# Third layer's attention: two pairs of score banks in turn, one bank each for the turned probabilities and the preparations

## The chip, the cores and the metric

One core of a Trainium2 chip runs the whole program. The metric is device microseconds of one execution, smaller is better. A core has TensorE (matmuls, which write only into PSUM), VectorE, ScalarE and GpSimd (called POOL in the profile), and SyncE (SP), each with its own queue of instructions; they wait for each other by semaphores. PSUM has eight banks of 512 fp32 values in each of 128 partitions, called 0 to 7 here.

## The reference

The model has four layers of attention and a mixture of experts on 32 batches of 128 tokens with 128 features; everything is fp32. The changed stage is the third layer's attention (`L2_xattn` in the reference, `latent_stage` in the kernel). Per batch, with `x` the 77 context tokens and `latents` the 128 tokens:

```
xn = layernorm(x, ln_x_g, ln_x_b)
ln = layernorm(latents, ln_l_g, ln_l_b)
q = ln @ Wq.T
kv = concatenate([xn @ Wkv.T, ln @ Wlkv.T], axis=1)      # 77 + 128 keys and values
q, k, v = split into 2 heads of 64
qn = rmsnorm(q, qn_g) * SCALE;  kn = rmsnorm(k, kn_g)
attn = einsum('bhid,bhjd->bhij', qn, kn)                 # masked for the 77
attn = softmax(attn, axis=-1)
out = einsum('bhij,bhjd->bhid', attn, v)
return out @ Wo.T + bo                                   # added to the tokens
```

In the same stage the kernel finishes the second layer's experts (gathers their rows, weighs, normalizes and adds them), and after the attention it normalizes the new tokens and computes the third router's logits.

## The kernel before, in words

The 32 batches are taken in eight turns of four. Each engine has its own program, a loop over iterations n from -12 to 38, written out by hand; t = n // 4 is the turn and i = n % 4 the place in it. Iterations below 0 are the head, in which only preparations run. The order of the calls in each loop is the order in that engine's queue; no planner changes it.

The steps of one batch n:

- `scores` (TensorE, iteration n-1): four matmul instructions of the heads' queries and keys into two banks, one head in each (line 1720), and four of the mask (line 1722). Each matmul of the program shows as two in the profile. It waits for `shift` of the batch before, since the two banks are the same for all batches.
- `maximum` and `shift` (VectorE, iteration n): the row maximum out of the score banks (line 1568), and the scores minus it into `soft` in SBUF (line 1572). After this the banks are free.
- `exponents` (ScalarE, n), `invert_sums` (VectorE, n+1, line 1579), `weigh` (ScalarE, n+1, line 1632).
- `turn_probs` (TensorE, n+2): four transposes of the weighted probabilities into one bank (lines 1731 and 1732), two banks in turn. `take_turned` (ScalarE, n+2) copies them out (lines 1638 and 1639).
- `values` (TensorE, n+3, lines 1741 and 1742), `take_attention` (ScalarE, n+3, line 1643), `project` (TensorE, n+3, line 1749), `add` (VectorE, n+3, line 1584), which adds the projection to the tokens.
- `keep_warm` (TensorE, line 1753): one matmul without use in each iteration.

Nine preparations of each turn, called jobs, run on TensorE between these steps, four batches at once. They share two banks in turn: job k uses bank k % 2 and waits until job k-2 has been copied out. In the queue's order they are x (transposes of the normalized tokens, line 1698; ScalarE copies them into `xT`, line 1598), r0 (query, key and value of the first batch, line 1709; ScalarE copies it into `raw`, line 1606), l (logits, line 1694; VectorE, line 1542), r1, r2, r3, k (transposes of the scaled keys, line 1704; VectorE copies them into `keys`, line 1545), q (queries of the four batches, line 1700; ScalarE, line 1601) and t (transposes of the finished tokens, line 1690; ScalarE, line 1596). The jobs x, r and q of a turn run two turns ahead of its attention, k one turn ahead; t and l follow one turn behind. So in turn t of the loop, x, r and q are those of turn t+2, and turns 6 and 7 have none. t and l begin in turn 2.

TensorE's loop, one iteration:

```
values(pe, n - 3)
for job in jobs_at(n, 0): do_job(pe, job)    # i = 2: x      i = 3: r2
turn_probs(pe, n - 2)
for job in jobs_at(n, 1): do_job(pe, job)    # i = 1: t      i = 2: r0, l      i = 3: r3, k
project(pe, n - 3)
scores(pe, n + 1)
keep_warm(pe)
for job in jobs_at(n, 2): do_job(pe, job)    # i = 2: r1     i = 3: q
```

VectorE's loop in one iteration: `maximum` and `shift` of n, at i = 3 `scale_keys` (line 1531, which k needs), `invert_sums` of n-1, at i = 0 the sums of squares (line 1520), at i = 1 `normalize` (line 1513, which x needs), `add` of n-3, the copies of its jobs, and then the rest of the second layer: `combine` (line 1459), `gain` (line 1476) and, at i = 3, `join` (line 1492). ScalarE's loop: `take_attention`, the copies of place 0, `take_turned`, the copies of place 1 (after r3 also the squares of the four batches, line 1610), `exponents`, `weigh`, the copies of place 2. POOL gathers rows by indirect DMAs and takes the reciprocal roots.

The eight banks before: 0 and 1 scores, 2 and 3 turned probabilities, 4 values, 5 projection, 6 and 7 preparations.

Of the kernel before, what the change touches and what calls it, by code (L numbers as in the profile page):

```python
# [15 lines left out]
ALU = mybir.AluOpType  # L16
ACT = mybir.ActivationFunctionType
AX_X = mybir.AxisListType.X

P = 128  # L20
NBATCH = 32
NTURN = NBATCH // 4
NKEY = 77
# [1344 lines left out]
def latent_stage(nc, net, latent, before, behind):  # L1368
# [6 lines left out]
    heads, NK, R = 2, NKEY + P, 4  # L1375

    with ExitStack() as ctx:  # L1377
        def sb(n, shape, dt=F32):
            return ctx.enter_context(nc.sbuf_tensor(f"L2x_{n}", shape, dt))

        def sem(n):
            return net.sem(f"L2x_{n}")

        x, ident = net.x, net.ident
        keys, wqkv = latent.keys, latent.wqkv
        score_ps = net.psum[:, 0:2, :]
        turn_bank, out_bank, proj_bank, prep_bank = net.banks[2:4], net.banks[4], net.banks[5], net.banks[6:8]

        got = [[sb(f"got{i}{k}", [P, 4, P]) for k in range(2)] for i in range(2)]
        y = sb("y", [P, 4, P]); ystats = sb("ystats", [P, 4, 6]); ymean_var = sb("ymean_var", [P, 4, 2]); yrstd = sb("yrstd", [P, 4])  # L1390
# [5 lines left out]
        qT = [sb(f"qT{i}", [P, 4 * P]) for i in range(2)]  # L1396
        soft = [sb(f"soft{i}", [P, heads, NK]) for i in range(4)]
        mx, rsum, rinv = ([sb(f"{n}{i}", [P, heads]) for i in range(2)] for n in ("mx", "rsum", "rinv"))
# [3 lines left out]
        E, wg = behind["E"], latent.wg  # L1402
# [8 lines left out]
        job_ps, keys_out, act_out = sem("job_ps"), sem("keys_out"), sem("act_out")  # L1411
        squared, summed, length_ready, chain3, scaled = (
            sem(n) for n in ("squared", "summed", "length_ready", "chain3", "scaled"))
        scores_ready, max_ready, shifted = sem("scores_ready"), sem("max_ready"), sem("shifted")
        exp_done, inv_ready, probs_ready = sem("exp_done"), sem("inv_ready"), sem("probs_ready")
        turned, turned_out, values_done = sem("turned"), sem("turned_out"), sem("values_done")
# [11 lines left out]
        def jobs_at(n, place):  # L1428
            t, i = n // 4, n % 4
            found = [(t + lag, j) for j, (lag, *at) in places.items() if at == [i, place] and 0 <= t + lag < NTURN]  # L1430
            if place == 1:
                found += [(d, what) for d in range(NTURN) for what, late in (("t", 3), ("l", 4)) if n == place_of(d) + late]
            return found

        HEAD, TAIL = -12, 7
        order = [job for n in range(HEAD, NBATCH + TAIL) for place in range(3) for job in jobs_at(n, place)]
        number = {job: k for k, job in enumerate(order)}

        def by_dve(job):
            return job[1] in ("k", "l")  # L1440

        def outs_by(job):

            some = [by_dve(j) for j in order[:number[job] + 1]]
            return sum(some), len(some) - sum(some)
# [89 lines left out]
        def take_job(dve, job):  # L1535
            if not by_dve(job):
                return
            t, what = job
            k = number[job]
            dve.wait_ge(job_ps, k + 1)  # L1540
            if what == "l":
                dve.tensor_copy(behind["logits"][:, :, 4 * t:4 * t + 4],
                                prep_bank[k % 2][:, 0:4 * E].rearrange("p (b e) -> p e b", b=4)).then_inc(keys_out, 1)
            else:
                dve.tensor_scalar(keys[:, 4 * t:4 * t + 4, NKEY:NK], prep_bank[k % 2][:, :].rearrange("p (b k) -> p b k", b=4),
                                  latent.gq[:, 0:1], latent.gk[:, 0:1], ALU.mult, ALU.mult).then_inc(keys_out, 1)

        def done_variances(dve, t):
# [16 lines left out]

        def maximum(dve, n):
            dve.wait_ge(scores_ready, n + 1)
            dve.tensor_reduce(mx[n % 2][:, :], score_ps[:, :, 0:NK], AX_X, ALU.max).then_inc(max_ready, 1)

        def shift(dve, n):  # L1570
            dve.wait_ge(max_ready, n + 1)
            dve.tensor_tensor(soft[n % 4][:, :, :], score_ps[:, :, 0:NK], mx[n % 2][:, :].unsqueeze(2).to_broadcast([P, heads, NK]),
                              ALU.subtract).then_inc(shifted, 1)

        def invert_sums(dve, n):
# [12 lines left out]
        def take_others(act, job):  # L1588
            if by_dve(job):
                return  # L1590
            t, what = job
            k = number[job]
            bank = prep_bank[k % 2]
            act.wait_ge(job_ps, k + 1)
            if what == "t":
                act.copy(lT[:, :], bank[:, :]).then_inc(act_out, 1)
            elif what == "x":
                act.activation(xT[:, :], bank[:, :], ACT.Identity, scale=latent.lat_g[:, 0:1],
                               bias=latent.lat_b[:, 0:1]).then_inc(act_out, 1)
            elif what == "q":  # L1600
                act.copy(qT[t % 2][:, :], bank[:, :]).then_inc(act_out, 1)
            else:
                b = int(what[1])
                if t >= R and b == 0:
                    act.wait_ge(values_done, 4 * (t - R + 1))
                act.copy(raw[t % R][:, b, :], bank[:, 0:3 * P]).then_inc(act_out, 1)
                if b == 3:
                    act.wait_ge(act_out, outs_by(job)[1])
                    act.wait_ge(summed, t)
                    act.activation(sq[:, :, :], raw[t % R][:, :, 0:2 * P], ACT.Square).then_inc(squared, 1)  # L1610
# [23 lines left out]

        def take_turned(act, n):
            act.wait_ge(turned, n + 1)
            ps = turn_bank[n % 2][:, :].rearrange("p (m t) -> p m t", m=4)
            act.copy(probs_lat[n % 2][:, :, :], ps[:, 0:2, :])
            act.copy(probs_ctx[n % 2][:, :, :], ps[0:NKEY, 2:4, :]).then_inc(turned_out, 1)

# [39 lines left out]
        def do_job(pe, job):  # L1680
            t, what = job
            k = number[job]
            if k >= 2:
                dve_outs, act_outs = outs_by(order[k - 2])
                pe.wait_ge(keys_out, dve_outs) if by_dve(order[k - 2]) else pe.wait_ge(act_out, act_outs)
            bank = prep_bank[k % 2]
            if what == "t":
                pe.wait_ge(normed2, t + 1)
                for b in range(4):
                    last = pe.transpose(bank[:, b * P:(b + 1) * P], behind["routed"].xn[:, 4 * t + b, :], ident[:, :])  # L1690
            elif what == "l":
                pe.wait_ge(act_out, outs_by((t, "t"))[1])
                for b in range(4):
                    last = pe.matmul(bank[:, b * E:(b + 1) * E], lT[:, b * P:(b + 1) * P], wg[:, :], start=True, stop=True)
            elif what == "x":
                pe.wait_ge(normed, t + 1)
                for b in range(4):
                    last = pe.transpose(bank[:, b * P:(b + 1) * P], xn[t % 2][:, b, :], ident[:, :])
            elif what == "q":
                last = pe.matmul(bank[:, :], wqkv[:, 0:P], xT[:, :], start=True, stop=True)  # L1700
            elif what == "k":
                pe.wait_ge(scaled, t + 1)
                for b in range(4):
                    last = pe.transpose(bank[:, b * P:(b + 1) * P], kn[:, b, :], ident[:, :])
            else:
                b = int(what[1])
                if b == 0:
                    pe.wait_ge(act_out, outs_by((t, "x"))[1])
                last = pe.matmul(bank[:, 0:3 * P], xT[:, b * P:(b + 1) * P], wqkv[:, :], start=True, stop=True)
            last.then_inc(job_ps, 1)  # L1710

        def scores(pe, n):
            t, b = n // 4, n % 4
            pe.wait_ge(shifted, n)
            if b == 0:
                pe.wait_ge(keys_out, outs_by((t, "k"))[0])
                pe.wait_ge(act_out, outs_by((t, "q"))[1])
            for i in range(heads):
                rows = slice(64 * i, 64 * i + 64)
                pe.matmul(score_ps[:, i, 0:NK], qT[t % 2][rows, b * P:(b + 1) * P], keys[rows, n, :], start=True, stop=False)  # L1720
            for i in range(heads):
                last = pe.matmul(score_ps[:, i, 0:NKEY], net.ones_row[:, :], latent.mask_row[:, n, :], start=False, stop=True)
            last.then_inc(scores_ready, 1)

        def turn_probs(pe, n):
            pe.wait_ge(probs_ready, n + 1)
            if n >= 2:
                pe.wait_ge(turned_out, n - 1)
            bank = turn_bank[n % 2]
            for i in range(heads):  # L1730
                pe.transpose(bank[:, i * P:(i + 1) * P], soft[n % 4][:, i, NKEY:NK], ident[:, :])
                last = pe.transpose(bank[0:NKEY, (2 + i) * P:(3 + i) * P], soft[n % 4][:, i, 0:NKEY], ident[:, :])
            last.then_inc(turned, 1)
# [1878 lines left out]
```

## Time and profile before

| | |
|---|---|
| time, median of 3 runs | 2423.79 us (2410.94, 2423.79, 2427.91) |
| profiled execution: span from first to last instruction | 2408.2 us |
| profiled execution: its own time | not marked among the three; the fastest lies 2.7 us above the span |
| TensorE matmuls, busy | 1980.2 us (82%) |
| VectorE, busy | 1543.5 us (64%) |
| ScalarE, busy | 1111.0 us (46%) |
| GpSimd, busy | 989.2 us (41%) |
| mean granted clock of TensorE | 0.916 of 2.4 GHz |

Busy shares are means over many stages with different limits; they don't say what binds the changed stage. Times in the profile's rows are microseconds from the start of the span, and a matmul's duration contains its way through the array, so that the durations of consecutive matmuls overlap.

### The profile page before, as it was taken

The page shows a single profiled execution, that of the slowest core. Times are in us where ns is not written, and L with a number is a line of the kernel's source. Part 1 is how long each engine was busy: PE and PEld are TensorE (multiplying, and loading weights), DVE is VectorE, ACT ScalarE, POOL GpSimd, SP SyncE. Part 2 cuts the span into 40 slices and gives each one's busy share as a digit, 9 for nine tenths or more (in the row PEclk, how much of TensorE's full clock was granted, in tenths as well). Part 3 has the DMA queues.
Part 4 walks back from the last instruction along what each step waited for, and adds up shares of the span by engine and source line. Part 5 has one row for each costly group of instructions (what it writes and reads, how often), then busy time and mean ns, then how long its engine had stood idle before and what let it go on. Part 6 is the DMA issues. An engine that isn't in the chain of part 4 may idle for free. (4 is left out here: it accounts for less than half of the span.)

```text
span 2408.2 us, 39264 instructions
## 1 busy us (share of the span) xinstructions
PE 1980.2 (82%) x14419; PEld 1400.9 (58%) x14419; DVE 1543.5 (64%) x3706; ACT 1111.0 (46%) x2201; POOL 989.2 (41%) x886
## 2 busy tenths in 40 slices
PE   5887799799999976854593898799589888879998
PEld 3666599667777754431592555567367566654443
DVE  6996522368787755969314885511598699866775
ACT  4886444244444432225331665423244567644443
POOL 3554165344443214647566741271675200112332
PEclk9997799899999988975796999899699999999999
DMA  3000478321112125979891100342231100012221
GB/s 113 1 2 2 146 242 245 103 70 59 59 56 75 37 67 178 327 255 309 264 325 53 26 12 1 128 126 78 68 122 49 41 2 2 2 36 75 80 80 48
DMA packets 138277, 238.45 MB, mean 99 GB/s; under 512 B 20755, under 2 KB 66748, under 8 KB 133970
## 3 DMA queue, kind: packets, MB, share of 16 engines
q1 hardware_dynamic: 114216, 173.65, 21.7%
q0 software_dynamic: 23872, 62.29, 9.2%
q8 instruction: 116, 1.90, 0.3%
q14 instruction: 73, 0.60, 0.1%
HBM read 161.89 MB, written 73.99 MB: 98 GB/s over the span
## 5 line engine op out<-in xcount | busy, mean ns | idle before, releaser
L432 POOL TENSOR_TENSOR L1x_soft<-L1x_soft,L1x_rinv 128x616 f32<-128x616 f32 x64 | 77.6, 1214 | 190.8 <-DVE L1x_rinv L355 190.7
L2153 ACT ACTIVATE L3f_hT<-banks,L3f_b 128x512 f32<-128x512 f32 x128 | 87.9, 687 | 136.9 <-PE banks L2172 130.1
L2098 DVE TENSOR_TENSOR L3f_hT<-L3f_hT,L3f_spread 128x512 f32<-128x512 f32 x128 | 99.8, 802 | 35.1 <-ACT L3f_hT L2153 32.7
L2185 PE MATMUL banks<-L3f_hT,L3f_w 128*128 128x512 f32 x256 | 121.4, 598 | 0.0
L2172 PE MATMUL banks<-L3f_xT,L3f_w 128*128 128x512 f32 x256 | 120.1, 593 | 0.6 <-PEq L730 0.6
L2663 POOL DMA_INDIRECT L0e_rows<-xn_rows,L0f_token_of x78 | 77.9, 999 | 98.0 <-issue 61.7
L887 POOL TENSOR_TENSOR L0x_soft<-L0x_soft,L0x_rinv 128x1232 f32<-128x1232 f32 x32 | 71.9, 2247 | 99.7 <-DVE L0x_rinv L812 99.7
L2982 ACT ACTIVATE L0e_hT<-banks,L0e_w 128x256 f32<-128x256 f32 x156 | 69.1, 473 | 88.3 <-PE banks L3025 88.3
L404 ACT COPY L1x_attnT<-banks 128x512 f32<-128x512 f32 x64 | 37.5, 585 | 148.2 <-PE banks L513 148.2
L2663 POOL DMA_INDIRECT L1h_rows<-xn_rows,L1f_token_of x72 | 73.9, 1026 | 77.8 <-POOLq L2416 46.7
L266 DVE COPY L1x_keys<-banks 128x308 f32<-128x308 f32 x112 | 52.0, 464 | 69.0 <-PE banks L461 68.9
L2663 POOL DMA_INDIRECT L2e_rows<-xn_rows,L2f_token_of x64 | 63.9, 999 | 69.6 <-POOLq L2416 39.4
L425 POOL DMA_INDIRECT L3x_got<-rows,L2f_slot_read x64 | 65.1, 1018 | 64.7 <-POOLq L61 49.0
L3339 POOL DMA_INDIRECT L1o_hid<-mixed,L1f_token_of x72 | 71.8, 997 | 44.0 <-issue 21.8
L2998 DVE TENSOR_TENSOR L0e_y<-banks,L0e_w 128x256 f32<-128x256 f32 x39 | 16.5, 424 | 114.3 <-PE banks L3034 114.3
L861 ACT COPY L3s_probsT<-banks 128x512 f32<-128x512 f32 x128 | 68.7, 591 | 44.3 <-PE banks L936 44.3
L485 PE MATMUL banks<-L1x_keys,L1x_xT 128*128 128x308 f32 x256 | 82.1, 443 | 7.4 <-DVE L1x_soft L346 6.7
L425 POOL DMA_INDIRECT L1x_got<-rows,L0f_slot_read x64 | 65.3, 1021 | 51.6 <-POOLq L61 36.2
L3208 POOL DMA_INDIRECT L1m_got<-hidden,L1f_slot_read x64 | 68.4, 1069 | 41.9 <-POOLq L3060 22.7
L461 PE MATMUL banks<-context,L1x_a 96*128 96x308 f32 x224 | 81.9, 448 | 4.2 <-DVE L1x_keys L266 4.2
L2172 PEld LDWEIGHTS banks<-L3f_xT,L3f_w 128*128 128x128 f32 x256 | 48.6, 190 | 61.5 <-issue 61.5
L1652 POOL DMA_INDIRECT L2x_got<-rows,L1f_slot_read x64 | 66.0, 1032 | 36.6 <-SPq L1377 19.4
(600 smaller groups left out, 5850.9 us busy)
## 6 DMA issues: line engine op xcount, KB each, us to landing
hidden<-L1h_hid SPq DMA_DIRECT2D x24, 768.0 KB, 5.0
L0e_w<-in_L0f_w SPq DMA_DIRECT2D x39, 320.0 KB, 4.7
L0e_w<-in_L0f_w SPq DMA_DIRECT2D x39, 258.0 KB, 3.8
L1x_flat_values<-L1x_staged SPq DMA_DIRECT2D x34, 256.0 KB, 2.0
L1x_vals<-L1x_flat_values SPq DMA_DIRECT2D x14, 616.0 KB
mixed<-L1m_out SPq DMA_DIRECT2D x32, 256.0 KB, 4.0
L3f_spread<-L3f_gates SPq DMA_DIRECT2D x8, 1024.0 KB, 7.4
L3x_keys<-L_keys SPq DMA_DIRECT2D x5, 1232.0 KB
```

The costliest lines, as they stand in the source:

```text
L425: pool.indirect_dma_start(got[g % 8][k][:, :], None, pre["rows"][:, :], bass.IndirectOffsetOnAxis(pre["routed"].read[:, g, k:k + 1], 0), b ...
L432: pool.tensor_tensor(tile, tile, rinv[n % 2][:, :].unsqueeze(2).to_broadcast([P, U, NK]), ALU.mult).then_inc(probs_ready, 1)
L461: last = pe.matmul(bank[:, 0:4 * NK], a[:, i, :], context[:, 4 * t:4 * t + 4, :], start=True, stop=True)
L485: last = pe.matmul(score_ps[:, i, 0:4 * NK], xT[t % 2][:, b * P:(b + 1) * P], keys[t % 2][:, U * u + 4 * i:U * u + 4 * i + 4, b, :], start ...
L887: pool.tensor_tensor(tile, tile, rinv[g % 2][:, :].unsqueeze(2).to_broadcast([P, heads, NK]), ALU.mult).then_inc(probs_ready, 1)
L2098: dve.tensor_tensor(tile, tile, spread[t % 2][:, e, :], ALU.mult).then_inc(weighed, 1)
L2153: act.activation(hT[m % 3][:, c, :], hid_bank[(FC * m + c) % 4][:, :], ACT.Relu, bias=b1[:, FC * e + c:FC * e + c + 1]).then_inc(hid_out, 1)
L2172: pe.matmul(hid_bank[n % 4][:, :], w1[:, e, c * P:(c + 1) * P], xT[t % 2][:, :], start=True, stop=True).then_inc(hid_ready, 1)
L2185: last = pe.matmul(bank[:, :], w2[:, e, c, :], hT[m % 3][:, c, :], start=False, stop=(e == E - 1 and c == FC - 1))
L2663: return pool.indirect_dma_start(out, None, net.xn_rows[:, :], bass.IndirectOffsetOnAxis(routed.token_of[:, tile:tile + 1], 0), bounds_che ...
L2982: act.activation(hT[j % 2][:, c, :], hid_bank[c][:, 0:Q * P], ACT.Gelu, bias=w1[j % R][:, FC * P + c:FC * P + c + 1]).then_inc(hid_out, 1)
L3339: pool.indirect_dma_start(hid[e % N][:, q, :], None, mixed_dram[:, :], bass.IndirectOffsetOnAxis(routed.token_of[:, Q * e + q:Q * e + q + ...
```

## The change

The two banks of the scores become two pairs, used by even and odd batches in turn (0 and 1, 2 and 3). `scores` of batch n now waits for `shift` of batch n-2 in place of n-1. In exchange the turned probabilities have one bank (4) in place of two, so that `turn_probs` of batch n waits until batch n-1 has been copied out, and the preparations have one bank (7) in place of two, so that each job waits until the job before it has been copied out. Values and projection move to banks 5 and 6. No computation is added, removed or moved in any queue.

```
-        score_ps = net.psum[:, 0:2, :]
-        turn_bank, out_bank, proj_bank, prep_bank = net.banks[2:4], net.banks[4], net.banks[5], net.banks[6:8]
+        score_ps = [net.psum[:, 0:2, 0:NK], net.psum[:, 2:4, 0:NK]]
+        turn_bank, out_bank, proj_bank, prep_bank = net.banks[4], net.banks[5], net.banks[6], net.banks[7]
...
-            dve.tensor_reduce(mx[n % 2][:, :], score_ps[:, :, 0:NK], AX_X, ALU.max).then_inc(max_ready, 1)
+            dve.tensor_reduce(mx[n % 2][:, :], score_ps[n % 2], AX_X, ALU.max).then_inc(max_ready, 1)
...
-            ps = turn_bank[n % 2][:, :].rearrange("p (m t) -> p m t", m=4)
+            ps = turn_bank[:, :].rearrange("p (m t) -> p m t", m=4)
...
-            if k >= 2:
-                dve_outs, act_outs = outs_by(order[k - 2])
-                pe.wait_ge(keys_out, dve_outs) if by_dve(order[k - 2]) else pe.wait_ge(act_out, act_outs)
-            bank = prep_bank[k % 2]
+            if k:
+                dve_outs, act_outs = outs_by(order[k - 1])
+                pe.wait_ge(keys_out, dve_outs) if by_dve(order[k - 1]) else pe.wait_ge(act_out, act_outs)
+            bank = prep_bank
...
-            pe.wait_ge(shifted, n)
+            if n >= 2:
+                pe.wait_ge(shifted, n - 1)
...
-                pe.matmul(score_ps[:, i, 0:NK], qT[t % 2][rows, b * P:(b + 1) * P], keys[rows, n, :], start=True, stop=False)
+                pe.matmul(score_ps[n % 2][:, i, :], qT[t % 2][rows, b * P:(b + 1) * P], keys[rows, n, :], start=True, stop=False)
...
-            if n >= 2:
-                pe.wait_ge(turned_out, n - 1)
-            bank = turn_bank[n % 2]
+            if n:
+                pe.wait_ge(turned_out, n)
+            bank = turn_bank
```

The lines left out change `shift`, `take_job`, `take_others` and the mask's matmuls to the same banks.

## Rows read from the trace of the kernel before

**Rows 1.** The page's chain of the work that ended last, by line.

```profile
PE banks L2185 5%; PE banks L2172 5%; PE banks L2182 0%; PE banks L2056 0%; PE banks L2192 0%; PE banks L2062 0%; PE banks L2048 0%; POOLq L3519 0%; POOL L3f_out_n L2136 0%; POOL L3f_out_n L2139 0%; POOL L3f_rstd L2131 0%; DVE L3f_stats L2110 0%; DVE L3f_out_n L2123 0%; DVE L3f_acc L2103 0%; ACT L3f_yT L2160 0%
```

**Rows 2.** Timeline: start, us, engine, line, operation, [idle before, releaser]; the stage's ends.

```profile
1290.44 0.61 DVE L1459 SCALAR_TENSOR_TENSOR L2x_y<-L2x_got,L1f_gate,L1f_xn_all 128x128 f32<-128x128 f32 x2 [16.67 <-DMA L2x_got<-rows,L1f_slot_read]
...
1508.84 2.02 PE L2357 MATMUL banks<-L3x_wqT,L3x_wkT 64*96 64x128 f32 x16 [0.60 <-PEq L1377]
```

**Rows 3.** List of waits, turn 0 (1325 to 1348.3): total, times, longest.

```profile
PE banks L1720 <- DVE L2x_soft L1572: 3.7, 2, 3.2
```

**Rows 4.** List of waits, turns 1 to 3 (1348.3 to 1413.5).

```profile
DVE x L1584 <- PE banks L1749: 7.0, 6, 1.5
...
PE banks L1720 <- DVE L2x_soft L1572: 2.4, 3, 1.2
```

**Rows 5.** List of waits, turns 4 to 7 (1413.5 to 1490).

```profile
PE banks L1720 <- DVE L2x_soft L1572: 0.4, 1, 0.4
```

**Rows 6.** Timeline of turn 3, iteration 2: r0, l, their copy, the addition.

```profile
1404.52 0.88 PE L1709 MATMUL banks<-L_wqkv,L2x_xT 128*128 128x384 f32 x2 [0.52 <-ACT L2x_xT L1598]
...
1405.24 0.95 PE L1694 MATMUL banks<-L_wg,L2x_lT 128*128 128x8 f32 x8
...
1405.44 0.48 ACT L1606 COPY L2x_raw<-banks 128x384 f32<-128x384 f32 x1 [0.54 <-PE banks L1709]
...
1406.55 0.29 DVE L1584 TENSOR_TENSOR x<-x,banks 128x128 f32<-128x128 f32 x1 [1.51 <-PE banks L1749]
```

**Rows 7.** Timeline of turn 3, iteration 3: r2's copy, r3, k, keys, join, scores.

```profile
1410.62 0.48 ACT L1606 COPY L2x_raw<-banks 128x384 f32<-128x384 f32 x1 [0.56 <-PE banks L1709]
...
1410.86 0.81 PE L1709 MATMUL banks<-L_wqkv,L2x_xT 128*128 128x384 f32 x2
...
1411.43 0.43 PEld L1704 LDWEIGHTS banks<-ident,L2x_kn 128*128 128x128 f32 x4 [0.38 <-ACT L2x_raw L1606]
...
1412.57 0.81 DVE L1545 TENSOR_SCALAR L_keys<-banks,L_gq,L_gk 128x512 f32<-128x512 f32 x1
...
1413.29 1.13 DVE L1492 SCALAR_TENSOR_TENSOR x<-L2x_y,L2x_yrstd,x 128x128 f32<-128x128 f32 x4
...
1413.48 0.62 PE L1720 MATMUL banks<-L_keys,L2x_qT 64*128 64x205 f32 x4 [1.15 <-issue]
```

**Rows 8.** Timeline of the head: the r jobs of turns 0 and 1, k, join.

```profile
1305.96 4.72 PE L1709 MATMUL banks<-L_wqkv,L2x_xT 128*128 128x384 f32 x8 [0.87 <-ACT L2x_xT L1598]
...
1307.65 0.48 ACT L1606 COPY L2x_raw<-banks 128x384 f32<-128x384 f32 x1 [1.74 <-PE banks L1709]
...
1312.32 1.22 DVE L1520 TENSOR_REDUCE L2x_length<-L2x_sq 128x16 f32<-128x1024 f32 x1 [1.18 <-ACT L2x_sq L1610]
...
1318.70 5.16 PE L1709 MATMUL banks<-L_wqkv,L2x_xT 128*128 128x384 f32 x8 [0.96 <-ACT L2x_xT L1598]
...
1323.45 0.60 PEld L1704 LDWEIGHTS banks<-ident,L2x_kn 128*128 128x128 f32 x4 [0.44 <-ACT L2x_raw L1606]
...
1324.34 0.81 DVE L1545 TENSOR_SCALAR L_keys<-banks,L_gq,L_gk 128x512 f32<-128x512 f32 x1 [3.55 <-PE banks L1704]
...
1325.07 2.94 DVE L1492 SCALAR_TENSOR_TENSOR x<-L2x_y,L2x_yrstd,x 128x128 f32<-128x128 f32 x4
```

**Rows 9.** Timeline of turn 0: `normalize` for x2, and x2's transposes.

```profile
1334.82 1.10 DVE L1513 TENSOR_SCALAR L2x_xn<-x,L2x_mean_var,L2x_rstd 128x128 f32<-128x128 f32 x4
...
1338.37 1.06 PE L1698 MATMUL banks<-ident,L2x_xn 128*128 128x128 f32 x4
```

**Rows 10.** Windows: stretch, length, busy us (instructions) by engine, granted clock, DMA.

```profile
1330.00:1341.00 11.00, 9.70 (x30) 5.96 (x30) 10.09 (x37) 4.14 (x13) 9.78 (x8) 0.53 0.10 25
1341.00:1415.00 74.00, 65.42 (x411) 42.74 (x410) 60.91 (x236) 50.98 (x151) 49.79 (x42) 1.00 0.10 24
1415.00:1419.00 4.00, 4.00 (x17) 2.06 (x16) 3.38 (x14) 0.85 (x2) 1.42 (x2) 0.57 0.00 0
...
1459.00:1463.40 4.40, 4.40 (x17) 2.23 (x17) 2.60 (x6) 1.27 (x4) 1.39 (x1) 0.61 0.00 0
```

More of the change, by code:

```diff
@@ L1542, in take_job @@
                 dve.tensor_copy(behind["logits"][:, :, 4 * t:4 * t + 4],
-                                prep_bank[k % 2][:, 0:4 * E].rearrange("p (b e) -> p e b", b=4)).then_inc(keys_out, 1)
+                                prep_bank[:, 0:4 * E].rearrange("p (b e) -> p e b", b=4)).then_inc(keys_out, 1)
             else:
-                dve.tensor_scalar(keys[:, 4 * t:4 * t + 4, NKEY:NK], prep_bank[k % 2][:, :].rearrange("p (b k) -> p b k", b=4),
+                dve.tensor_scalar(keys[:, 4 * t:4 * t + 4, NKEY:NK], prep_bank[:, :].rearrange("p (b k) -> p b k", b=4),
                                   latent.gq[:, 0:1], latent.gk[:, 0:1], ALU.mult, ALU.mult).then_inc(keys_out, 1)
@@ L1567, in maximum @@
             dve.wait_ge(scores_ready, n + 1)
-            dve.tensor_reduce(mx[n % 2][:, :], score_ps[:, :, 0:NK], AX_X, ALU.max).then_inc(max_ready, 1)
+            dve.tensor_reduce(mx[n % 2][:, :], score_ps[n % 2], AX_X, ALU.max).then_inc(max_ready, 1)
         def shift(dve, n):
             dve.wait_ge(max_ready, n + 1)
-            dve.tensor_tensor(soft[n % 4][:, :, :], score_ps[:, :, 0:NK], mx[n % 2][:, :].unsqueeze(2).to_broadcast([P, heads, NK]),
+            dve.tensor_tensor(soft[n % 4][:, :, :], score_ps[n % 2], mx[n % 2][:, :].unsqueeze(2).to_broadcast([P, heads, NK]),
                               ALU.subtract).then_inc(shifted, 1)
@@ L1682, in do_job @@
             k = number[job]
-            if k >= 2:
-                dve_outs, act_outs = outs_by(order[k - 2])
-                pe.wait_ge(keys_out, dve_outs) if by_dve(order[k - 2]) else pe.wait_ge(act_out, act_outs)
-            bank = prep_bank[k % 2]
+            if k:
+                dve_outs, act_outs = outs_by(order[k - 1])
+                pe.wait_ge(keys_out, dve_outs) if by_dve(order[k - 1]) else pe.wait_ge(act_out, act_outs)
+            bank = prep_bank
             if what == "t":
@@ L1719, in scores @@
                 rows = slice(64 * i, 64 * i + 64)
-                pe.matmul(score_ps[:, i, 0:NK], qT[t % 2][rows, b * P:(b + 1) * P], keys[rows, n, :], start=True, stop=False)
+                pe.matmul(score_ps[n % 2][:, i, :], qT[t % 2][rows, b * P:(b + 1) * P], keys[rows, n, :], start=True, stop=False)
             for i in range(heads):
-                last = pe.matmul(score_ps[:, i, 0:NKEY], net.ones_row[:, :], latent.mask_row[:, n, :], start=False, stop=True)
+                last = pe.matmul(score_ps[n % 2][:, i, 0:NKEY], net.ones_row[:, :], latent.mask_row[:, n, :], start=False, stop=True)
             last.then_inc(scores_ready, 1)
```

## The prediction

> **What bounds the kernel now.** I read the page first. Its chain of the work that ended last has 5% each on lines 2172 and 2185, the last layer's experts, and no line of the changed stage [rows 1]; of this stage it says nothing. What matters is that the stage is closed: VectorE begins it after a wait of 16.67 us for the gathered rows, and the next stage's first matmuls at 1508.84 come after a barrier [rows 2]. Every microsecond that the stage loses or gains should reach the end unchanged.
>
> Inside the stage I read the list of waits, cut by turns (four batches each), and then the timeline. TensorE waits for VectorE's shift ahead of the score matmuls: 3.7 us in turn 0, 2.4 us in turns 1 to 3, 0.4 us afterwards, 6.5 us in all in six places [rows 3 to 5]. That is all that a second pair of score banks can remove. The same list has two waits that stay. Ahead of the first scores of a turn TensorE stands 1.15 us, because they need the keys that VectorE has just copied; the row [rows 7] stands for seven, turns 1 to 7. And VectorE stands ahead of its addition at line 1584 until TensorE's projection is done, 7.0 us in turns 1 to 3 [rows 4]: at iterations 2 and 3 of a turn TensorE is the late one, and any delay of a projection is handed to VectorE.
>
> **The score banks: what is removed.** In turns 1 to 5 the removed waits are 2.4 + 0.4 = 2.8 us. The work queued behind them (the next transposes, the copy into xT, r0) follows on TensorE and ends in the addition for which VectorE waited 1.51 us [rows 6], so I count the 2.8 us in full. The wait of scores n+1 for shift n becomes one for shift n-1. That is already implied: the transposes of batch n-2 earlier in TensorE's order need the weighted probabilities, which need the reciprocal behind shift n-1. So no wait replaces it. In turn 0 the 3.7 us are worth less, as the matter of the first turn shows below. DMAs and the queues of SP and POOL are not touched.
>
> **The turned bank: nothing.** Transposing batch n-2 now waits until batch n-3 has been copied out. The value matmuls of batch n-3, which stand ahead of it in the same iteration, wait for the same copy. Without that cover it would cost one pair of ScalarE copies.
>
> **The preparation bank: what is added.** A turn has nine jobs, in the order x, r0, l, r1, r2, r3, k, q, t. Each now waits for the copy of the one before it. Six of the waits I count at nothing: r0 already needs the copy of x as data; q comes behind the first scores, which need the copy of k; r1, t and x have scores, keep-warm matmuls and values between them and the job before, which cover a copy; and r2 loaded its weights in the same hundredths in which r1's copy ended. Three stand too close.
>
> l: r0's copy runs from 1405.44 to 1405.92, and l's first matmul started at 1405.24 [rows 6]. It can start some 0.1 us after the copy, so 0.8 us late; the projection behind it, and VectorE's addition, follow. l meets an r0 in turns 2 to 5: 4 x 0.8 = 3.2 us.
>
> r3 and k: r2's copy ends at 1410.62 + 0.48 = 1411.10, and r3's matmuls started at 1410.86 [rows 7], so r3 moves by 0.35 us to 1411.2. They take 0.81, the copy 0.48: it ends at about 1412.55, and k's weights, which loaded at 1411.43, load at 1412.6. k is late by 1.2 us. Behind k stand the projection, then VectorE's addition, then the copy of the keys (0.81 us, from 1412.57), then the first scores at 1413.48 [rows 7]. All are in one chain, so turn after turn starts 1.2 us later: five times in turns 1 to 5, 6.0 us, and once in turn 0. Turns 6 and 7 have no r jobs and lose nothing.
>
> The turns 1 to 5 together: 6.0 + 3.2 - 2.8 = +6.4 us.
>
> The head runs two sets of jobs with nothing between them. A cold pass from r00's first matmul to the end of its copy is 1305.96 to 1308.13, 2.17 us [rows 8]; a warm one, r0 in turn 3, 1404.52 to 1405.92, 1.40 us [rows 6]. First set: four passes end at 1305.96 + 4 x 2.17 = 1314.6, with two warm ones at 1313.1; before, the run ended at 1310.68 and its last copy about 0.5 later. That is +3.5 or +1.9; I take +3.0. It goes on through the squares, for which VectorE waited 1.18 us [rows 8]. Second set: from r10 to k's weights it was 1318.70 to 1323.45, 4.75 us; four cold passes take 8.7, two cold and two warm 7.1: +3.9 or +2.4. Its eight matmuls took 5.16 us, 0.645 each, all cold, so I take +3.5. VectorE waited 3.55 us for k there [rows 8], so this passes on too. Then its joining step took 2.94 us, against 1.13 us in a turn [rows 7, 8]; moved by 6 us it may lose that disturbance, -1.8 to 0; I take -1.5, as 1.13 is its size in the turns. VectorE enters turn 0 late by 3.0 + 3.5 - 1.5 = 5.0 us (2.5 to 7.4).
>
> The first turn has the slack of the removed score waits. The transposes of x2 started at 1338.37; their input was ready at 1334.82 + 1.10 = 1335.92 [rows 9]. With the score waits gone only that input holds them: 1335.92 + 5.0 = 1340.9, +2.5 us (0 to 4.9). With k's 1.2 us turn 0 costs +3.7.
>
> **Clock.** The granted clock was 0.53 between 1330 and 1341 and fell to 0.57 and 0.61 for about 4 us in two places, the first just behind a 1.15 us wait at the first scores of a turn; between 1341 and 1415, with three such waits in it, it was 1.00 [rows 7, 10]. One fall costs some 4.00 x (1 - 0.57) = 1.7 us. The waits of l, r3 and k add gaps around those places; I take one fall more, +1.7 us, bounds -3.4 (none left) to +8.5 (five more). The Trainium skill (TensorE: Matmul & The Clock Gate, Part 1) says that activity releases the throttle and idleness brings it back. By that alone every turn would have to fall; the rows show two.
>
> Sum: 3.7 + 6.4 + 1.7 = 11.8 us. The profiled execution's span is 2408.2 us, 2.7 below the fastest of the three runs and 15.6 below their median; which run it was is not marked. As the sum is a difference, I set it on the median: 2423.8 + 11.8 = 2436 us.
>
> A rule speaks against the half that gives up banks. The Trainium skill (Perfetto Trace Analysis, Optimizing Tensor Performance) wants independent matmul groups to rotate through banks, so that copying one out overlaps the next group's matmuls. By it each of the nine jobs pays its copy; it is the third rival.
>
> **Rivals.** Low clock: the added gaps keep TensorE at 1.2 GHz through half of each of turns 0 to 5. For: the falls follow waits. Against: seven turns start after 1.15 us, two fall. Price: about 10 us a turn at 0.57, 4.3 each, 26 in all above the 10.1 without falls: 2460.
>
> Full clock, which ends not slower: the early scores fill turn 0 and the gaps, and TensorE is granted 2.4 GHz from the head on. The head's passes then take 1.40: the first set ends 0.4 late, the second gains 0.85, the join gives back 1.8, so x2 is no longer late but up to 3.0 early, the half-speed work up to 1341 shrinks by 1.2, and both falls vanish (-3.4). With +1.2 and +6.4 this is 0.0: 2424. It decides if VectorE's first maximum comes no later than in the old trace. Against: the second set of the head ran dense and still cold.
>
> Every copy exposed: nine copies at 0.48, 4.3 us a turn instead of 2.0, because ScalarE comes late to each. In turns 0 to 5 that is 14 us more: 2450. Against: ScalarE stood idle ahead of the copy of r0 [rows 6].
>
> The change does not do what it says: the early scores only move the wait to the next transposes. Then the 2.8 us stay lost: 2439, inside the range.
>
> **How the numbers follow.** Forecast 0.68, low clock 0.10, full clock 0.12, every copy exposed 0.04, wait only moved 0.06. The forecast's own bounds are 0 + 1.2 + 6.4 - 3.4 = +4 and 4.9 + 1.2 + 6.4 + 8.5 = +21, 2428 to 2445; the runs of one kernel spread over 17 us, so half of that goes to either side: 2420 to 2453, which also takes in the full clock's 2424 and the exposed copies' 2450 and leaves out the low clock. One per cent, 24 us, is about what a measurement here can tell. Slower by more than that: 2448 and above, low clock 0.10, exposed copies 0.03, the forecast's upper edge 0.05: 0.18. Faster by over 1% needs a gain of which the six waits hold a quarter: 0.02. The rest, 0.80, is within.
>
> **What would show it.** No wait of line 1720 for line 1572 in turns 1 to 7. Waits of l's, r3's and k's weight loads for ScalarE's line 1606, 0.8, 0.4 and 0.8 us. The copies of the head's r jobs 2.2 us apart instead of 1.28 or less. VectorE's first maximum about 5 us later against the stage's start, the first scores of turn 6 about 10 to 12 us later, and the stage's last two turns as long as before. I am wrong if the clock in the stage is granted otherwise than here, or if VectorE, not TensorE, turns out to set iterations 2 and 3, so that a delayed k costs less than it is late.

## The result and the profile after

The changed kernel takes 2441.14 us (median of 4 runs, 2436.81 to 2445.82) against 2425.24 us for the kernel before in the same session (2410.94 to 2427.91): a ratio of 1.0082, 95% interval 1.0062 to 1.0103. By this interval it is slower by 15 to 25 us, by the medians 15.9: inside the forecast range, and more than the forecast 11.8.

The profiled execution of the changed kernel took 2445.82 us with a span of 2444.0, the longest of its four; that of before, by its span of 2408.2, was the shortest of its own. So I read the stage by itself, from VectorE's first combine to the next stage's first matmuls (before: [rows 2]). Behind line 1713 the numbers are one higher than before. Timeline of the changed kernel (columns as in [rows 2]), the two ends of the stage:

```profile
1296.41 0.61 DVE L1459 SCALAR_TENSOR_TENSOR L2x_y<-L2x_got,L1f_gate,L1f_xn_all 128x128 f32<-128x128 f32 x2 [16.77 <-DMA L2x_got<-rows,L1f_slot_read]
...
1540.49 2.02 PE L2358 MATMUL banks<-L3x_wqT,L3x_wkT 64*96 64x128 f32 x16 [0.59 <-PEq L1377]
```

That is 244.1 us where it was 218.4 [rows 2], 25.7 more. The list of waits of the changed kernel from 1340 to 1526 (releaser, total, times, longest) has none of the scores (now line 1721) for line 1572 any more; the 1.15 us ahead of the first scores of each turn have stayed, and three new ones have come:

```profile
DVE x L1584 <- PE banks L1750: 46.6, 23, 5.3
...
PE banks L1721 <- issue: 8.0, 7, 1.1
...
PEld banks L1704 <- ACT L2x_raw L1606: 7.1, 6, 1.2
...
PEld banks L1694 <- ACT L2x_raw L1606: 4.7, 4, 1.2
...
PEld banks L1709 <- ACT L2x_raw L1606: 2.4, 8, 0.4
```

k waits in six turns, l in the four in which it meets an r0, and r2 and r3 0.3 us each, all for ScalarE's copy: the places that the forecast named, and r2 besides. The first line shows where it ends: VectorE stands longer ahead of its addition. The same line of the kernel before, from 1326 to 1494, the same part of its stage:

```profile
DVE x L1584 <- PE banks L1749: 29.9, 20, 3.7
```

Head of the changed kernel, timeline (before: [rows 8]):

```profile
1314.21 1.65 PE L1709 MATMUL banks<-L_wqkv,L2x_xT 128*128 128x384 f32 x2 [0.57 <-ACT L2x_raw L1606]
...
1315.90 0.48 ACT L1606 COPY L2x_raw<-banks 128x384 f32<-128x384 f32 x1 [1.74 <-PE banks L1709]
...
1318.12 0.48 ACT L1606 COPY L2x_raw<-banks 128x384 f32<-128x384 f32 x1 [1.74 <-PE banks L1709]
...
1321.93 1.22 DVE L1520 TENSOR_REDUCE L2x_length<-L2x_sq 128x16 f32<-128x1024 f32 x1 [5.07 <-ACT L2x_sq L1610]
...
1338.32 0.81 DVE L1545 TENSOR_SCALAR L_keys<-banks,L_gq,L_gk 128x512 f32<-128x512 f32 x1 [7.94 <-PE banks L1704]
1339.05 1.13 DVE L1492 SCALAR_TENSOR_TENSOR x<-L2x_y,L2x_yrstd,x 128x128 f32<-128x128 f32 x4
```

The copies come 2.22 us apart. The sums of squares start 25.5 us behind the stage's start instead of 21.9, the keys 41.9 instead of 33.9, and VectorE's first maximum, at 1341.61, 45.2 instead of 39.0.

The clock tells the rest. Windows of the kernel before over its head (columns as in [rows 10]), a stretch that the prediction did not use:

```profile
1308.44:1316.44 8.00, 3.29 (x7) 1.13 (x6) 6.58 (x28) 3.18 (x6) 6.39 (x7) 0.92 0.12 34
1316.44:1322.44 6.00, 4.82 (x10) 2.78 (x11) 4.17 (x19) 1.73 (x3) 5.07 (x5) 0.51 0.16 44
1322.44:1329.44 7.00, 4.12 (x17) 2.00 (x16) 4.99 (x15) 3.88 (x5) 4.32 (x4) 0.93 0.15 37
1330.44:1340.44 10.00, 9.14 (x29) 5.70 (x29) 9.68 (x36) 3.62 (x12) 8.78 (x8) 0.50 0.11 28
```

The same part of the changed kernel, up to the point where its clock rises:

```profile
1314.41:1322.41 8.00, 6.29 (x8) 1.81 (x8) 2.82 (x15) 2.49 (x4) 6.57 (x7) 0.50 0.12 33
1322.41:1335.41 13.00, 6.99 (x12) 2.69 (x12) 7.68 (x31) 2.92 (x6) 8.36 (x9) 0.50 0.14 36
1335.41:1361.70 26.29, 24.71 (x70) 13.25 (x70) 16.90 (x56) 10.54 (x27) 15.73 (x13) 0.50 0.10 22
```

Before, the clock rose to 2.4 GHz within the last microsecond of each dense run of eight r matmuls [rows 8], and 50 us behind the stage's start the clock rose for the turns. With 0.57 us of waiting ahead of every pair of them it stays at 1.2 GHz for the whole head and most of turn 0, until 65 us behind the start (58 us in the repeat below). Windows of the changed kernel by turns (first scores to first scores; the last one ends with the stage):

```profile
1339.21:1365.61 26.40, 24.57 (x76) 13.75 (x76) 17.14 (x58) 12.51 (x34) 14.58 (x12) 0.57 0.09 20
1365.61:1386.81 21.20, 18.85 (x114) 11.69 (x115) 17.92 (x72) 14.20 (x44) 15.79 (x13) 1.00 0.11 26
1386.81:1411.71 24.90, 21.95 (x126) 13.60 (x127) 19.08 (x77) 14.90 (x45) 15.74 (x13) 0.93 0.09 22
1411.71:1438.21 26.50, 23.59 (x126) 14.19 (x126) 19.29 (x77) 14.69 (x45) 13.53 (x11) 0.87 0.08 16
1438.21:1463.11 24.90, 21.93 (x126) 13.65 (x127) 19.30 (x77) 14.76 (x45) 7.20 (x5) 0.93 0.00 1
1463.11:1489.61 26.50, 23.58 (x126) 14.10 (x126) 14.39 (x54) 14.71 (x45) 6.67 (x4) 0.87 0.00 1
1489.61:1509.31 19.70, 18.03 (x114) 11.75 (x114) 11.09 (x36) 11.80 (x40) 5.80 (x3) 0.91 0.01 1
1509.31:1540.51 31.20, 24.11 (x174) 17.39 (x174) 13.24 (x56) 14.30 (x48) 2.08 (x3) 0.93 0.00 1
```

Length times (1 - clock) is what a turn would have been shorter at full clock if TensorE's work alone set its length; I call it the low clock's share, and an upper bound. In turns 1 to 6 it is 12.0 us here (turn 3: 26.50 x 0.13 = 3.4) and was 3.4 in the same view of before. Read in windows of 1 us, these are seven falls of 3.4 us each at 1.2 GHz where before had two of the same length [rows 10]: four begin 1.1 to 2.1 us behind the first scores of turns 3 to 6, three some 16 to 18 us into turns 2, 3 and 5, within 2 us behind l.

### The profile page after: what moved, and what is told of

Same layout as the page of the kernel before. It is cut to its first block and busy times, and to the rows that moved or that the text cites. A ratio compares the mean times of both kernels' runs of the same rounds, so it can differ in the third digit from the quotient of the medians.

```text
span 2444.0 us, 39266 instructions
## 1 busy us (share of the span) xinstructions
PE 2011.3 (82%) x14419; PEld 1411.7 (58%) x14419; DVE 1544.4 (63%) x3706; ACT 1111.3 (45%) x2201; POOL 987.0 (40%) x886
## 5 line engine op out<-in xcount | busy, mean ns | idle before, releaser
L425 POOL DMA_INDIRECT L3x_got<-rows,L2f_slot_read x64 | 65.2, 1019 | 64.7 <-POOLq L61 49.0
L425 POOL DMA_INDIRECT L1x_got<-rows,L0f_slot_read x64 | 65.3, 1021 | 54.9 <-POOLq L61 39.5
L3209 POOL DMA_INDIRECT L1m_got<-hidden,L1f_slot_read x64 | 67.8, 1060 | 41.2 <-POOLq L3061 21.9
L3026 PE MATMUL banks<-L0e_xT,L0e_w 128*128 128x256 f32 x312 | 78.0, 395 | 4.2 <-DMA L0e_w<-in_L0f_w 4.1
```

The costliest lines, as they stand in the source:

```text
L425: pool.indirect_dma_start(got[g % 8][k][:, :], None, pre["rows"][:, :], bass.IndirectOffsetOnAxis(pre["routed"].read[:, g, k:k + 1], 0), b ...
L3026: pe.matmul(hid_bank[c][:, 0:Q * P], w1[j % R][:, c * P:(c + 1) * P], xT[j % 2][:, :], start=True, stop=True).then_inc(hid_ready, 1)
```

## The experiments

All stages are measured from the first combine; "falls" are returns to 1.2 GHz in turns 1 to 6 (in turn 7 every kernel has some, 5 to 16 us long in all up to the end of the stage). Theory A says that the handovers of the single preparation bank cost some 10 us by themselves and that the gaps they open cost at least as much again through the clock. The main rival says that the handovers alone are the cost and the falls cost nothing; a second, that the halved turned bank or the score pairs do it.

**Pairs alone.** Score pairs and one turned bank as in the change, but two preparation banks; to find the room, projections go to the output's bank, and the keep-warm matmuls write to the turned bank:

```
turn_bank, out_bank, proj_bank, prep_bank = net.banks[4], net.banks[5], net.banks[5][:, P:2 * P], net.banks[6:8]
```

> The two pairs of score banks are kept, the preparations have their two banks again; values and projection share a bank, and the keep-warm matmuls write into the bank of the turned probabilities. Theory A (the loss comes from the preparations' single bank, and from the lower clock that its gaps bring; the pairs and the single turned bank are harmless): the stage, 218.4 us from the first combine to the next stage's matmuls before and 244.1 us after, comes to 213 to 218 us, the run is 0 to 6 us faster than before, and TensorE doesn't wait for the shift (line 1572) ahead of the scores. Rival B (running the scores ahead itself disturbs the stage: VectorE or the clock): the stage stays above 228 us and the run is 10 us or more slower than before.

2416.8 against 2420.26 us, ratio 0.9984 [0.9968, 0.9999]; stage 217.7 us, first maximum 38.9, two falls. One wait for the shift, of 1.23 us, is left, in turn 0. Half of the change costs nothing and gains a little; the turned bank is cleared of suspicion.

**One preparation bank alone.** The kernel before, with this half of the change:

```
-            if k >= 2:
-                dve_outs, act_outs = outs_by(order[k - 2])
...
-            bank = prep_bank[k % 2]
+            if k:
+                dve_outs, act_outs = outs_by(order[k - 1])
...
+            bank = prep_bank
```

> Only the preparations lose a bank; scores and turned probabilities are as before. Theory A: the whole loss of the change and the small gain missing, a stage of 240 to 250 us, 15 to 25 us slower than before. Rival B: a stage under 228 us, less than 8 us slower.

2445.64 us, ratio 1.0111 [1.0085, 1.0137]; stage 248.8, first maximum 45.1, seven falls, four of them of 6.8 us. The whole loss is here.

The next three keep both banks and add the wait for the job before to some jobs only, so that its parts can be told apart.

**Head alone:** jobs of the two sets ahead of the turns wait as in the change.

```
for late in ((1, 2) if (t == 0 and what != "t" and what != "l") or (t == 1 and what in ("x", "r0", "r1", "r2", "r3", "q")) else (2,)):
```

> The kernel before with both preparation banks, but in the head (the jobs x, r0 to r3, q of turns 0 and 1, and k of turn 0) each job also waits for the copy of the job before. Theory A (handovers add up, and a head that is not dense leaves TensorE at 1.2 GHz longer): first maximum 6 us later against the stage's start, the first scores of turn 1 10 to 12 us later, the stage 226 to 231 us. Rival C (the handovers alone count, the clock recovers as before): first maximum 6 us later, but the slack of turn 0 takes some of it, so turn 1 is 4 to 6 us later and the stage is 222 to 225 us.

2424.88 us, ratio 1.0023 [1.0007, 1.0040]; stage 229.5, first maximum 45.2, first scores of turn 1 at 65.2 us instead of 57.8. The clock is 0.50 through the head here too, until 59 us behind the start: the head's waits hold it down, and nothing in the turns does. Theory A's first maximum and stage came; turn 1 came 7.3 us later, between its 10 to 12 and rival C's 4 to 6.

**r2, r3 and k alone:**

```
for late in ((1, 2) if (t >= 2 and what in ("r2", "r3")) or (t >= 1 and what == "k") else (2,)):
```

> The kernel before with both preparation banks, but from the loop on the jobs r2, r3 (of turns 2 to 7) and k (of turns 1 to 7) also wait for the copy of the job before. Theory A as forecast (1.2 us in each of turns 0 to 5): 7 us, a stage of 225 to 226 us, with two or three falls of the clock. Rival D (the gaps bring falls of the clock, 1.7 us each, in most turns): 12 to 17 us, a stage of 230 to 236 us, and five or more falls.

2434.56 us, ratio 1.0070 [1.0043, 1.0096]; stage 238.0, six falls, one of them of 6.8 us: a low clock's share of 12.0 us for the 3.4 of before, the same in its repeat below. Rival D's falls came, and its 236 us were passed. Without the low clock's share (half of the time at 1.2 GHz, here and below) turns 0 to 5 take 131.5 us against 125.9 and 126.2 in the two executions of before: 5.3 to 5.6 us for the forecast's 1.2 x 6 = 7.2, and 4.1 to 4.5 of it in turns 1 to 5.

**The gaps filled at l, r3 and k.** The changed kernel with a useless matmul ahead of each (of 256 columns; in the head of 128, ahead of r1 and r2 too):

```
+            if what in ("l", "r3", "k") or (n < 0 and what in ("r1", "r2")):
...
+                pe.matmul(out_bank[:, P:(1 + c) * P], ident[:, :], ident[:, :].unsqueeze(1).to_broadcast([P, c, P]), start=True, stop=True)
```

> The changed kernel as it is, but ahead of l, r3 and k (in the head also r1 and r2) TensorE runs one matmul without use (256 columns; 128 in the head) into the values' bank, in the time in which it would wait for the copy. Theory A, with the falls of the clock as the larger part of the loss: the clock falls in two or three of the turns 1 to 7 in place of seven, and the stage is 226 to 236 us in place of 244.1; the 6 us of the three handovers in the turns stay. Rival C (the falls have another cause, the handovers are dearer than they look): six or more falls, a stage of 243 us or more.

2437.21 us, ratio 1.0064 [1.0043, 1.0084]; stage 241.0, five falls. A miss for both: most falls stayed, and the stage lies between the two. Read by place, though, four of the five now begin within 2 us behind the first scores of a turn, whose 1.15 us wait had not been filled, and only one behind l.

**l alone:**

```
for late in ((1, 2) if what == "l" else (2,)):
```

> The kernel before with both preparation banks, but the job l also waits for the copy of the job before it. Theory A: 0.8 us in each of the turns 2 to 5, a stage of 221 to 222 us with the two falls that there were, 3 us over the kernel before; one fall more would make it 224. Rival: it is hidden behind VectorE, 218 to 219 us.

2429.57 us, ratio 1.0024 [1.0010, 1.0039]; stage 230.0, three falls, some 17 us into turns 2, 3 and 4, just behind l, two of them of 6.8 us. The stage is well above the expected 221 to 222, but not for l's own wait: without the low clock's share turns 1 to 5 take 111.6 us against 108.0 and 108.4 before, so 3.1 to 3.5 us for the forecast 3.2. The rest is mostly falls, which l's wait brings besides, and 1.4 to 1.5 us of the head, which runs ahead of the first l and in which the clock was low for 10.2 us in place of 6.8 between the two r runs.

**Pairs alone, first scores filled.** One line into the version with pairs alone:

```
             if b == 0:
+                keep_warm(pe, n - 1)
                 pe.wait_ge(keys_out, outs_by((t, "k"))[0])
```

> The run with the pairs alone, and one keep-warm matmul more (384 columns) ahead of the first scores of each turn, where TensorE waits 1.15 us for the keys. Theory A (the falls come behind this wait): at most one fall in the turns 1 to 7, a stage of 210 to 214 us, 5 to 9 us faster than before. Rival: the wait isn't what the clock falls for, 216 to 219 us, as without.

2412.8 against 2421.1 us, ratio 0.9964 [0.9951, 0.9978]; stage 215.7, above the expected 210 to 214, and no fall. This version beats both kernels. What the filling alone adds to the pairs alone is not clear of noise: the two ratios' intervals overlap, and of the two falls that went only one had begun behind the first scores.

**The kernel before again.**

> The kernel before, profiled once more, to see how far the stage and its falls differ between two executions. Theory A: the stage within 3 us of 218.4, with one to three falls in the turns 1 to 7, and the head and turn 0 the same to 0.5 us. Rival: the stage differs by 8 us or more, so that a single profile of it can't carry the experiments.

2421.6 us; stage 223.3, two falls and a longer one in turn 7. The stage of one kernel differs by 4.9 us between two executions, more than the 3 us expected; most of that is the low clock's share over turns 0 to 7, 12.5 and 16.7 us.

**The changed kernel with its first scores filled,** and **the changed kernel again.** The edit is the line above, as `keep_warm(pe)`.

> The changed kernel with one keep-warm matmul more ahead of the first scores of each turn. Theory A (in turns 1 to 7 the change costs three handovers plus falls of the clock, and a matmul in the wait of the first scores stops the falls): no fall in turns 1 to 7, the stage shrinks from 244 us to 228 to 234 us; what is left above the 215.7 us of the version with pairs alone and the same filling is the head (5 us at the first maximum), the later x2 of turn 0 and the handovers (about 2 us a turn). Rival B (handovers alone, the falls cost nothing): the stage stays at 240 to 246. Rival C (the change's falls start at l, r3 and k and the filling doesn't reach them): four or more falls stay, 238 to 244.

> The changed kernel again, one look, for the spread of its stage from run to run: 236 to 246 us (244.1 in the first profile), first maximum 45 us behind the stage's start, 5 to 8 falls in turns 1 to 7. If the stage is under 236, the first profile was an extreme one and its excess over the forecast is chance.

The first: 2435.57 us against 2418.68, ratio 1.0066 [1.0049, 1.0083]; stage 240.2. Theory A's number missed, rival C's fits: the falls behind the first scores are gone and four are left, one in each of turns 2 to 5, three of them of 6.8 us, so that the low clock's share of turns 1 to 6 is 12.0 us as in the first profile. Timeline of this version, TensorE in turn 2:

```profile
1389.88 0.88 PE L1709 MATMUL banks<-L_wqkv,L2x_xT 128*128 128x384 f32 x2 [0.52 <-ACT L2x_xT L1598]
1391.33 1.15 PE L1694 MATMUL banks<-L_wg,L2x_lT 128*128 128x8 f32 x8 [0.57 <-ACT L2x_raw L1606]
1392.33 0.78 PE L1751 MATMUL banks<-L_wo,L2x_attnT 128*128 128x128 f32 x2
1393.04 1.05 PE L1722 MATMUL banks<-L_keys,L2x_qT 64*128 64x205 f32 x4
```

r0 has waited 0.52 us for the copy of x, as it did before [rows 6], and l 0.57 for the copy of r0; two matmuls of the projection then take 0.78 us instead of the 0.39 of full clock. The second: 2444.78 us, stage 248.8, above the expected 246, so the long stage of the first profile is no accident. Both profiled executions of the changed kernel lie near the upper end of its runs, though (2436.81 to 2445.82), and its median run may have a shorter stage.

**Filled ahead of r0 and l as well,** and **everywhere at once:**

```
+            if n >= 0 and what in ("r0", "l"):
...
+                pe.matmul(out_bank[:, P:(1 + c) * P], ident[:, :], ident[:, :].unsqueeze(1).to_broadcast([P, c, P]), start=True, stop=True)
```

This condition is that of the first; the second's takes in r3 and k too, and r1, r2, r3 and k of the head. Both fill the first scores.

> The version with the filled first scores, and one useless matmul of 256 columns more ahead of r0 and of l in the turns. With the first scores filled, four falls were left, one in each of turns 2 to 5, each within 5 us behind l, in the turns in which l waits 0.57 us right behind r0's wait of 0.52 us. Theory A2 (this pair of waits sets those falls off): no fall or one in turns 2 to 5, each of these turns 23 to 24 us instead of 24.9 to 26.4, the stage 230 to 235 us. Rival C2 (the falls of turns 2 to 5 come from the sum of the added waits, l's, r3's and k's, wherever they lie): three or four falls stay or move to r3 and k, the stage 239 to 243.

> The changed kernel with useless matmuls ahead of every waiting place at once: the first scores, r0, l, r3 and k of the turns and r1, r2, r3 and k of the head. Theory A (clock): no fall in turns 1 to 7; the stage 229 to 236 us, where what is left above the 215.7 us of the version with pairs alone and filled is the handovers themselves and the fillers that lie on the path. Rival C (waits at the handovers and not the clock are the cost): still 238 us or more with no fall left. Rival D (the clock falls without regard to such waits): four or more falls left.

2426.5 us, ratio 1.0035 [1.0016, 1.0054], stage 231.0; and 2425.77 us, ratio 1.0015 [0.9999, 1.0032], stage 229.9. One fall is left in each, in turn 4. Windows of the first of the two, turns 2 to 5:

```profile
1373.87:1397.17 23.30, 21.92 (x134) 13.77 (x134) 19.09 (x77) 14.86 (x45) 15.78 (x13) 1.00 0.10 23
1397.17:1420.47 23.30, 21.92 (x134) 13.77 (x134) 19.28 (x77) 14.87 (x45) 13.66 (x11) 1.00 0.08 18
1420.47:1445.27 24.80, 23.46 (x132) 14.43 (x132) 19.08 (x77) 14.84 (x45) 7.20 (x5) 0.93 0.01 1
1445.27:1468.57 23.30, 21.92 (x132) 13.77 (x132) 14.27 (x54) 14.74 (x45) 6.68 (x4) 1.00 0.00 1
```

With useless work added, turns 2, 3 and 5 are 3.1 us shorter each than with the first scores alone filled (26.4). Theory A is borne out, and the rival that the falls cost nothing is refuted. Filling r3, k and the head too changes the stage by 1 us: with the waits of r0, l and the first scores filled, those of r3 and k bring no falls of their own.

They are not harmless for that. Falls that begin within 2.2 us behind the first scores of turns 1 to 6 number two, one, one, two and none in the five versions whose r2, r3 and k don't wait in the turns (before twice, pairs alone, head alone, l alone), and four, five, four, five and four in the five whose do (the changed kernel twice, one preparation bank alone, r2, r3 and k alone, l, r3 and k filled). The 1.15 us wait is in all ten; more falls follow it where these jobs wait ahead of it, and in all four versions that fill it no such fall is left. At l it is the added wait: with l alone made to wait, three of turns 2 to 5 have a fall behind it. r0 and l were filled only together, so that what filling one of them would do beside filled first scores is not shown.

## Why the prediction was right in direction and too small

The terms of the sum against the stage, twice: the first profiles, and the two repeats. Each is a difference of the stretch's length, with the low clock's share of turns 1 to 7 taken out into rows of its own. The stage was longer by 25.7 and 25.5 us in these pairs of executions, the medians of the runs by 15.9; so the rows show where the loss lies, and more of it than a median run has.

| term | forecast | 244.1 - 218.4 | 248.8 - 223.3 |
|---|---|---|---|
| to the first scores of turn 1 | 3.7 | 11.4 | 8.6 |
| turns 1 to 5 without low clock | 6.4 | 5.8 | 5.0 |
| turns 6 and 7 without low clock | 0 | 1.7 | 0.0 |
| low clock, turns 1 to 6 | 1.7 | 8.5 | 12.0 |
| low clock, turn 7 | 0 | -1.7 | -0.1 |
| sum | 11.8 | 25.7 | 25.5 |

**Right: the handovers.** l, r3 and k wait where forecast, the projection and VectorE's addition follow, and turns 1 to 5 without the low clock come out at 5.0 to 5.8 us for 6.4. In part that is luck, since two of its terms were too large and have opposite signs. l alone measured 3.1 to 3.5 for 3.2. r3 and k measured 4.1 to 4.5 for 6.0. The score pairs were counted at 2.8 us there; the version with pairs alone shows 1.4 to 1.8 (106.6 for 108.0 and 108.4 us), and there the shared output bank and its wait are included. The parts add up: one preparation bank alone takes 115.5 us there, 7.1 to 7.5 more than before. No wait took the place of the shift's, and the turned bank cost nothing. The rival of nine exposed copies is out: only l, r2, r3 and k show an added wait in the turns. The Trainium skill (Perfetto Trace Analysis, Optimizing Tensor Performance) wants groups to rotate through banks; the head agrees, where a pass takes 2.22 us between copies instead of the 1.28 that it took at the same low clock with two banks.

**Right in size: the head.** First set +3.6 for 3.0; keys +8.0, so +4.4 in the second part for 3.5; the join took 1.13 instead of 2.94 us, -1.8 for -1.5; VectorE's first maximum +6.2 for 5.0, within 2.5 to 7.4.

**Wrong: the first turn.** The step "with the score waits gone only that input holds them", +2.5 for x2's transposes, failed. They started at 1350.33, 53.9 us behind the start instead of 47.9: +6.0. Their input accounts for +3.8 of that, since the first maximum came 6.2 us late and not 5.0. But it was not the input that held them, as the changed kernel's timeline shows:

```profile
1346.99 1.10 DVE L1513 TENSOR_SCALAR L2x_xn<-x,L2x_mean_var,L2x_rstd 128x128 f32<-128x128 f32 x4
...
1348.89 1.65 PE L1754 MATMUL banks<-ident 128*128 128x384 f32 x2
...
1350.33 1.06 PE L1698 MATMUL banks<-ident,L2x_xn 128*128 128x128 f32 x4
```

The input was there at 1348.09, and TensorE came 2.24 us after it. The join's gain is VectorE's alone; TensorE began turn 0 when the keys came, 8.0 us late, and its first scores and the queries behind them now ran at half speed. Before, then after:

```profile
1325.25 0.62 PE L1720 MATMUL banks<-L_keys,L2x_qT 64*128 64x205 f32 x4 [0.95 <-issue]
...
1326.39 1.12 PE L1700 MATMUL banks<-L2x_xT,L_wqkv 128*128 128x512 f32 x2
...
1330.69 1.05 PE L1720 MATMUL banks<-L_keys,L2x_qT 64*128 64x205 f32 x4 [3.18 <-DVE L2x_soft L1572]
```

```profile
1339.18 1.05 PE L1721 MATMUL banks<-L_keys,L2x_qT 64*128 64x205 f32 x4 [0.91 <-DVE L_keys L1545]
...
1341.23 2.08 PE L1700 MATMUL banks<-L2x_xT,L_wqkv 128*128 128x512 f32 x2
...
1343.23 1.05 PE L1721 MATMUL banks<-L_keys,L2x_qT 64*128 64x205 f32 x4
```

From its first scores to x2's transposes TensorE needed 13.12 us before, 3.68 of them waits for the shift, and 11.15 after, without a wait: 3.68 us of waits removed were worth 1.97. Where the clock was back in time the step held: in the version with r0 and l filled the queries took 1.13 us, and x2 started 0.14 us behind its input. Behind x2 come the other 5.4 of the 11.4 us, 1.2 of them forecast for k: the half-speed stretch lasted 15 us longer than before (9 in the repeat). I had taken the head as cold in the old kernel and read its clock only from 1330 on; it had two stretches at full clock, the second up to the first scores and queries of turn 0, and the change removed both. That the clock is granted otherwise than in the rows was one of my own signs of being wrong. With all gaps filled the clock was back 38 us behind the start, and turn 1 came 4.8 us late, close to the forecast 3.7. With the same head and only l, r3 and k filled it was back as early, but low again for 10.2 us from 51 us on, and turn 1 came 7.7 us late.

**Wrong: "I take one fall more, +1.7 us".** That term measured 8.5 and 12.0 us. The price of a fall was right, 1.7 us for 3.4 us at half speed. Their number was not: five more in the first profile, exactly the bound of +8.5 that I had put at the edge, and in the repeat seven falls of which two are twice as long. With it the stage's 25.7 and 25.5 us lie above my own upper bound of +21; that the time lies well inside the range is owed to the median run, which lost 15.9, and there is luck in that. The low-clock rival, with its price of 26 us, named the mechanism; a third to a half of it happened, and in other places, at the first scores and behind l. The Trainium skill (TensorE: Matmul & The Clock Gate, Part 1) says that idleness brings the throttle back. The trace agrees on the direction: pairs of waits of 0.52 and 0.57 us were followed by falls, and filling them took three of four away. That one follows every wait, as I had read it, is not so: in the changed kernel turn 1, with its waits at the first scores and at k, stayed at 1.00.

**Open.** Why the fall of turn 4 stays with every place filled; why the falls behind the first scores stayed with l, r3 and k filled; and why the clock rises 42 us behind the start in the version with r0 and l filled but at 57 us with the first scores alone filled, although TensorE's program is the same up to there (the changed kernel itself had 65 and 58). The 6.0 us by which the changed kernel reached the stage later are not the change's: the unchanged work ahead of it ended between 1288.8 and 1298.2 in these executions.

## What to carry to other kernels

A buffer taken from a dense TensorE run was paid twice here, once for the copy that is exposed and once for the clock: read the granted clock over every stretch that the buffer serves, the head of the stage included, before pricing the gap. A wait that is removed is worth its length only if the work around it keeps its clock: here 3.68 us of waits bought 1.97. Where a wait can't be removed, a useless matmul into free columns of a bank is worth a trial, but at all the places that bring a fall: filling one of two left most of the loss in place.

## What was unexpected of the hardware

Waits of 0.57 us between pairs of matmuls of 1.65 us kept the clock at 1.2 GHz for the whole head, where the same eight matmuls without waits had it at 2.4 GHz before they ended. A fall in turns 1 to 6 had a length of 3.4 us in most places and of 6.8 us in some, and took 1.7 or 3.4 us from its turn. And fillers are cheap: ahead of r0 and l they cost turns 2, 3 and 5 some 0.3 us each (23.3 us measured, against 26.4 - 26.4 x 0.13 = 23.0 without them and without the low clock).
